# Gathered sums of a graph network: eight slots in the ring, addresses of a visit ahead of its waits

## The chip, the cores and the metric

The kernel runs on one core of a Trainium2 chip. The metric is the device time of one execution in microseconds (us), measured without the profiler; lower is better.

## The reference, cut to what matters

Four graph networks stand one behind the other on 3125 nodes with 256 features each, every one with a residual and a layer norm. The change touches the third, three relational layers over 18750 edges of 8 types:

```python
def _rgcn_layer(x, W, root, bias, src, dst, seg):
    agg = jax.ops.segment_sum(x[src], seg, num_segments=N_REL * N_NODES)
    agg = agg.reshape(N_REL, N_NODES, -1)
    return jnp.einsum('rnd,rde->ne', agg, W) + x @ root + bias
seg = edge_type * N_NODES + dst
h = x
for l in range(N_LAYERS - 1):
    h = jax.nn.relu(_rgcn_layer(h, weights[l], roots[l], biases[l], src, dst, seg))
h = jax.nn.sigmoid(_rgcn_layer(h, weights[-1], roots[-1], biases[-1], src, dst, seg))
```

## The kernel before, in words

**What a layer does.** For each node the products with all eight type matrices are written to a table in HBM; one row of the table is 3 x 256 bfloat16 values (a number split in three pieces). A layer then walks over the sorted edges in 25 tiles of 128 target nodes. For each chunk of 128 edges, GpSimd (POOL) gathers 128 table rows of 768 values with an indirect DMA (L2653), and TensorE (PE) multiplies them by a 0/1 matrix `hot` that DVE builds, so that the products add up in PSUM over the edges of a target node. Four chunks make a group, and a group of rows fills one slot of a ring `rows` of `R = SLOTS = 4` slots; `hot` and `lane` have a ring of the same length. `gather_sum` is called three times: `rel0s` and `rel1s` also compute the next layer's table while they sum (`then`), `rel2s`, the last, has only the sums.

**Counts.** 168 groups of four gathers in each layer, 672 gathers. A group whose edges end in one tile and begin in the next is used by both, so PE makes 191 visits of a group in a layer: 168 `add` and 23 `again`.

**Who waits for whom.** POOL waits, ahead of each group, for the group's indices (`s_at`, L2648, from DVE) and for the slot (`s_used`, L2649, from PE); L2650 stands behind both waits. With four slots group n may be gathered once PE has begun the visit of group n-3. SP waits for the 64 increments of each slot's semaphore and counts `s_landed` up by one (L2641). DVE computes row numbers (L2670, behind `s_landed`), target lanes (L2678) and `hot` (L2681), adds the finished tile (L2701, L2703), and prepares the next table (L2708, L2713, L2718), all in program order. PE visits a group: it waits for `s_hot` and `s_landed`, and issues for each of the four chunks a matmul of 512 columns (L2785) and one of 256 (L2788). Slots come from registers, so each operand needs its address worked out by PE's sequencer ahead of the matmul: in the order these are the rows `ISA` without a tile, in the trace the rows `FUSED_REGOPS`. In `rel0s` and `rel1s` PE puts between a visit's chunks the products for the next table (L2834) and, between tiles, sums counted edges (L3209, L3210) and closes each with a one-column matmul (L2814, L3211).

Of the kernel before, what the change touches and what calls it, by code (L numbers as in the profile page):

```python
# [6 lines left out]
P = 128  # L7
N = 3125
D = 256
# [22 lines left out]
SLOTS = 4  # L32
PIECES = 3
# [2559 lines left out]
def gather_sum(nc, name, g, table, own, out=None, then=None):  # L2593

    B, R = G_SUM, SLOTS
    WIDE = (REL + 1) * D
    NC = REL // 2
    with Phase(nc, name) as ph:
        rows = ph.sb("rows", [P, R, B, PIECES * D], BF16)
# [43 lines left out]
        @block.gpsimd  # L2643
        def _(pool):
            turns = turns_of(pool, g)
            with pool.Fori(0, turns, 1) as i:
                for u in range(R):
                    pool.wait_ge(s_at, i * R + (u + 1))  # L2648
                    pool.wait_ge(s_used, i * R + (u + 1))  # L2649
                    pool.sem_inc(g.waited, 1)  # L2650
                    for k in range(B):
                        n = u * B + k
                        pool.indirect_dma_start(rows[:, u, k, :], None, table,  # L2653
                                                bass.IndirectOffsetOnAxis(ap=at[:, n:n + 1], axis=0)).then_inc(s_in[u], 16)
# [108 lines left out]
        def _(pe):  # L2763
# [17 lines left out]
            def visit(a, hot_slot, row_slot, fresh, ends, after=None):  # L2781
                for k in range(B):
                    to = hot[:, bass.ds(hot_slot, 1), :, k].rearrange("p a n -> p (a n)")
                    row = rows[:, bass.ds(row_slot, 1), k, :].rearrange("p a d -> p (a d)")
                    one = nc.tensor.matmul(acc[a][:, :], to, row[:, 0:2 * D], start=fresh and k == 0, stop=False)  # L2785
                    if k == 0 and ends:
                        one.then_inc(s_used, 1)
                    last = nc.tensor.matmul(acc[a][:, D:2 * D], to, row[:, 2 * D:3 * D], start=False, stop=False)  # L2788
# [6 lines left out]
            def again(a):  # L2795
                v = pe.snap(seen, min_val=0, max_val=most)
                hot_slot = pe.snap(v % R)
                q = pe.snap(rows_in, min_val=0, max_val=most)
                row_slot = pe.snap((q + (R - 1)) % R)
                pe.wait_ge(s_hot, v + 1)  # L2800
                visit(a, hot_slot, row_slot, True, False)

            def add(a, fresh=False, after=None):
# [3 lines left out]
                row_slot = pe.snap(q % R)  # L2807
                pe.wait_ge(s_hot, v + 1)
                pe.wait_ge(s_landed, q + (R + 1))
                visit(a, hot_slot, row_slot, fresh, True, after)  # L2810
# [417 lines left out]
def program(nc, x, src, dst, kind, noise, gcn, local, ssm, mix, rel, last, out):  # L3228
    ctx = ExitStack()
    with ctx:  # L3230
# [45 lines left out]
        g.pool_sems = [ctx.enter_context(nc.semaphore(f"pool_dma{n}")) for n in range(36)]  # L3276
# [74 lines left out]
```

## Time and profile before

| | us |
|---|---|
| median of 3 timed runs | 7024.69 |
| lowest and highest of them | 7013.26, 7026.6 |
| span of the profiled execution | 7499.8 |

The profiled execution is one run with the recorder on; nothing of the program lies outside its span, so its own time is the 7499.8 us. It is 475.1 us longer than the median of the timed runs. Of the span PE is busy for 4435.1 us, DVE for 4012.2 us, POOL for 2382.3 us and ACT for 1792.5 us. The three relational sums take from 3515 to about 6640 us. A row's idle time is that of its engine just before it, and behind the arrow stands what ended it; "issue" is time in which the engine waited for nothing that the profile shows. PEld is the load of weights on TensorE, PEldq and POOLq are the instruction sequencers of these engines.

### The profile page before, as it was taken

How to read it: one execution, taken by the hardware profiler on the slowest of the kernel's cores; microseconds unless marked ns; L12 is line 12 of the kernel's file. 1: busy time of each engine (PE TensorE's matmuls, PEld its weight loads, DVE VectorE, ACT ScalarE, POOL GpSimd, SP SyncE). 2: the span in 40 equal slices, each digit the busy share in tenths (PEclk: the TensorE clock that was granted, in tenths of full speed). 3: DMA queues.
4: the chain of work that ended last, by engine and by line, in shares of the span. 5: the costliest groups of instructions: out<-in, count | busy, mean ns of one | idle time of the engine just before them, and what ended most of it. 6: DMA issues, size and time to landing. Idle time of an engine off the chain costs nothing. (4 is left out here: it accounts for less than half of the span.)

```text
span 7499.8 us, 87742 instructions
## 1 busy us (share of the span) xinstructions
PE 4435.1 (59%) x18992; PEld 2329.9 (31%) x19133; DVE 4012.2 (53%) x6257; ACT 1792.5 (24%) x2729; POOL 2382.3 (32%) x2285
## 2 busy tenths in 40 slices
PE   4888566217992554788456775556774444430583
PEld 2454465103441222654223332223331122220221
DVE  8986475898996695554222332223331111128895
ACT  1575112006882321443001111001110000010352
POOL 0000000400000353101666665666656666620000
PEclk8999687558995787899777887777886666665896
DMA  1471664326663575145555555555664444443443
GB/s 41 159 235 39 222 245 158 140 92 181 181 180 94 192 262 204 59 156 198 155 163 177 192 192 167 166 160 184 194 185 144 135 137 139 137 129 123 140 134 108
DMA packets 487888, 1181.10 MB, mean 157 GB/s; under 512 B 65242, under 2 KB 272293, under 8 KB 475138
## 3 DMA queue, kind: packets, MB, share of 16 engines
q1 hardware_dynamic: 313518, 570.19, 23.1%
q0 software_dynamic: 140880, 464.72, 20.5%
q10 hardware_dynamic: 33396, 145.09, 5.3%
q8 instruction: 41, 0.67, 0.0%
q14 instruction: 53, 0.43, 0.0%
HBM read 914.86 MB, written 268.11 MB: 158 GB/s over the span
## 5 line engine op out<-in xcount | busy, mean ns | idle before, releaser
L2653 POOL DMA_INDIRECT rel1s_rows<-rel_table,rel1s_at x672 | 652.1, 970 | 408.7 <-issue 345.7
L2653 POOL DMA_INDIRECT rel0s_rows<-rel_table,rel0s_at x672 | 653.7, 973 | 380.4 <-issue 346.6
L2653 POOL DMA_INDIRECT rel2s_rows<-rel_table,rel2s_at x672 | 648.1, 964 | 372.3 <-issue 333.1
L2785 PE MATMUL rel2s_acc<-rel2s_rows,rel2s_hot 128*128 x753 | 393.8, 537 | 469.6 <-issue 412.3
L2126 POOL TENSOR_TENSOR mamb_st<-mam_u,mamb_bc 128x1600 f32<-128x1600 f32 x64 | 230.8, 3606 | 1135.7 <-DMA mamb_bc<-dbc 1135.7
L1677 PE MATMUL gatx_acc<-gatx_w,gatx_feat 128*65 128x400 f32 x1600 | 541.6, 501 | 25.3 <-DVE gatx_w L1569 25.3
L2785 PE MATMUL rel0s_acc<-rel0s_rows,rel0s_hot 128*128 x740 | 332.8, 466 | 302.0 <-issue 212.6
L2785 PE MATMUL rel1s_acc<-rel1s_rows,rel1s_hot 128*128 x702 | 315.9, 464 | 275.9 <-issue 209.2
L1569 DVE SCALAR_TENSOR_TENSOR gatx_w<-gatx_w,gatx_adj 128x1600 f32<-128x1600 f32 x200 | 363.9, 1820 | 0.5 <-ACT gatx_w L1625 0.5
L1416 DVE CUSTOM_DVE_ANT_0 gatm_junk<-gatm_srow,gatm_gone 128x3200 bf16<-128x3200 f32 x100 | 343.5, 3489 | 33.5 <-DMA gatm_srow<-gat_scores 29.1
L1677 PE MATMUL latx_acc<-latx_w,latx_feat 128*65 128x400 f32 x800 | 291.3, 508 | 102.0 <-DVE latx_w L1569 102.0
L2171 PE MATMUL mamb_acc<-mamb_st,g_ident 128*128 128x512 f32 (+1 forms) x512 | 239.9, 623 | 150.5 <-DVE mamb_st L2159 150.5
L1677 PEld LDWEIGHTS gatx_acc<-gatx_w,gatx_feat 128*65 128x65 f32 x1600 | 221.2, 138 | 342.4 <-issue 315.6
L2678 DVE TENSOR_SCALAR rel2s_lane<-g_dsts,g_tile_base x168 | 43.0, 256 | 525.9 <-remote 392.3
L2788 PE MATMUL rel2s_acc<-rel2s_rows,rel2s_hot 128*128 x764 | 276.9, 362 | 67.0 <-issue 64.6
L438 PE MATMUL adj_acc<-adj_high,adj_low 128*128 x1196 | 269.3, 349 | 67.3 <-DVE adj_high L395 59.7
L2785 PEld LDWEIGHTS rel2s_acc<-rel2s_rows,rel2s_hot 128*128 x764 | 97.9, 128 | 660.2 <-issue 644.9
L395 DVE TENSOR_TENSOR adj_high<-adj_num,adj_mine 128x1600 f16 x299 | 296.2, 991 | 0.0
L2788 PE MATMUL rel1s_acc<-rel1s_rows,rel1s_hot 128*128 x764 | 245.1, 321 | 53.8 <-issue 44.0
L2678 DVE TENSOR_SCALAR rel1s_lane<-g_dsts,g_tile_base x168 | 40.6, 242 | 440.7 <-DMA dbc<-mamad_dbc 294.1
L2788 PE MATMUL rel0s_acc<-rel0s_rows,rel0s_hot 128*128 x764 | 244.7, 320 | 37.5 <-issue 35.2
L2678 DVE TENSOR_SCALAR rel0s_lane<-g_dsts,g_tile_base x168 | 42.5, 253 | 417.5 <-remote 224.3
(611 smaller groups left out, 9605.8 us busy)
## 6 DMA issues: line engine op xcount, KB each, us to landing
mamb_bc<-dbc SPq DMA_DIRECT2D x128, 800.0 KB, 5.8
agg_strip<-strips SPq DMA_DIRECT2D x100, 800.0 KB, 5.5
gatx_adj<-adj SPq DMA_DIRECT2D x200, 400.0 KB, 3.0
adj<-adj_counts SPq DMA_DIRECT2D x25, 1600.0 KB, 7.1
latx_adj<-adj SPq DMA_DIRECT2D x100, 400.0 KB, 3.0
rel_table<-rel0p_prod POOLq DMA_DIRECT2D x25, 1536.0 KB, 6.2
rel_table<-rel0s_prod ACTq DMA_DIRECT2D x25, 1536.0 KB
rel_table<-rel1s_prod ACTq DMA_DIRECT2D x25, 1536.0 KB
```

What stands on the lines that cost most here:

```text
L395: nc.vector.tensor_tensor(slot_of(high, slot).rearrange("p a k n q -> p (a k) n q"), num1[:, :, :].unsqueeze(1).to_broadcast([P, Q // 2, W ...
L438: last = nc.tensor.matmul(bank[:, 0:W16], low[:, bass.ds(slot, 1), :, i].rearrange("p a n -> p (a n)"), high[:, bass.ds(slot, 1), i // 2, ...
L1416: last = nc.vector.tensor_tensor_reduce(out=junk[:, h, :], in0=srow[:, h, :], in1=gone[u][:, :], scale=1.0, scalar=-3e38, op0=ALU.subtract ...
L1569: nc.vector.scalar_tensor_tensor(w[u][:, :, :], w[u][:, :, :], 1.0, adj[u][:, :].unsqueeze(1).to_broadcast([P, 2, J]), ALU.min, ALU.mult). ...
L1677: last = nc.tensor.matmul(acc[k][h][:, a, 0:J // 2], feat[u][:, h * 65:(h + 1) * 65], w[u][:, h, a * (J // 2):(a + 1) * (J // 2)], start=F ...
L2126: nc.gpsimd.tensor_tensor(st[q % RS][:, :], u[:, ct, when(half)], bc[r % RB][:, :], ALU.mult).then_inc(s_x, 1)
L2171: last = nc.tensor.matmul(acc[:, a:b], g.ident[:, :], st[q % RS][:, a:b], start=False, stop=n == S - 1)
L2653: pool.indirect_dma_start(rows[:, u, k, :], None, table, bass.IndirectOffsetOnAxis(ap=at[:, n:n + 1], axis=0)).then_inc(s_in[u], 16)
L2678: nc.vector.tensor_scalar(mine.rearrange("p a q -> p (a q)"), g.dsts[:, bass.ds(chunk, B)], base, None, ALU.subtract).then_inc(s_lane, 1)
L2785: one = nc.tensor.matmul(acc[a][:, :], to, row[:, 0:2 * D], start=fresh and k == 0, stop=False)
L2788: last = nc.tensor.matmul(acc[a][:, D:2 * D], to, row[:, 2 * D:3 * D], start=False, stop=False)
```

## The change

`SLOTS` goes from 4 to 8, so the rings of rows, indices, lanes and `hot` have eight slots, POOL's and SP's loops have eight groups in a turn (21 turns instead of 42), and 48 semaphores for DMAs are made instead of 36. The four chunks of a slot now lie in four tensors `rows0` to `rows3` instead of one. PE works out all addresses of a visit, four for the 512-column operands, four for the 256-column ones and four for `hot`, in one block ahead of the visit's two waits; the matmuls then follow each other with nothing between.

```diff
-SLOTS = 4
+SLOTS = 8
...
-        rows = ph.sb("rows", [P, R, B, PIECES * D], BF16)
+        rows = [ph.sb(f"rows{k}", [P, R, PIECES * D], BF16) for k in range(B)]
...
-                        pool.indirect_dma_start(rows[:, u, k, :], None, table,
+                        pool.indirect_dma_start(rows[k][:, u, :], None, table,
...
-            def visit(a, hot_slot, row_slot, fresh, ends, after=None):
+            def operands(hot_slot, row_slot):
+                of_row = lambda k: rows[k][:, bass.ds(row_slot, 1), :].rearrange("p a d -> p (a d)")
+                hots = [hot[:, bass.ds(hot_slot, 1), :, k].rearrange("p a n -> p (a n)") for k in range(B)]
+                most_two = [of_row(k)[:, 0:2 * D] for k in range(B)]
+                least = [of_row(k)[:, 2 * D:3 * D] for k in range(B)]
                 for k in range(B):
-                    to = hot[:, bass.ds(hot_slot, 1), :, k].rearrange("p a n -> p (a n)")
-                    row = rows[:, bass.ds(row_slot, 1), k, :].rearrange("p a d -> p (a d)")
-                    one = nc.tensor.matmul(acc[a][:, :], to, row[:, 0:2 * D], start=fresh and k == 0, stop=False)
+                    nc.tensor.lower_ap(most_two[k])
+                for k in range(B):
+                    nc.tensor.lower_ap(least[k])
+                for k in range(B):
+                    nc.tensor.lower_ap(hots[k], for_matmul_weights=True)
+                return hots, most_two, least
+
+            def visit(a, of_visit, fresh, ends, after=None):
+                hots, most_two, least = of_visit
+                for k in range(B):
+                    one = nc.tensor.matmul(acc[a][:, :], hots[k], most_two[k], start=fresh and k == 0, stop=False)
...
-                    last = nc.tensor.matmul(acc[a][:, D:2 * D], to, row[:, 2 * D:3 * D], start=False, stop=False)
+                    last = nc.tensor.matmul(acc[a][:, D:2 * D], hots[k], least[k], start=False, stop=False)
...
+                of_visit = operands(hot_slot, row_slot)
                 pe.wait_ge(s_hot, v + 1)
                 pe.wait_ge(s_landed, q + (R + 1))
-                visit(a, hot_slot, row_slot, fresh, True, after)
+                visit(a, of_visit, fresh, True, after)
...
-        g.pool_sems = [ctx.enter_context(nc.semaphore(f"pool_dma{n}")) for n in range(36)]
+        g.pool_sems = [ctx.enter_context(nc.semaphore(f"pool_dma{n}")) for n in range(48)]
```

On PE, one visit in the loop over a tile's groups in the last layer (`add`) reads before as follows; ISA is a register operation, REGISTER_ALU the one that makes the number waited for, so the first matmul stands behind the waits and two operations behind that row.

```order
L2804 ISA
L2809 REGISTER_ALU
L2785 ISA x2
L2785 MATMUL rel2s_acc1<-rel2s_rows,rel2s_hot 128x512
L2788 ISA
L2788 MATMUL rel2s_acc1<-rel2s_rows,rel2s_hot 128x256
L2785 ISA
L2785 MATMUL rel2s_acc1<-rel2s_rows,rel2s_hot 128x512
L2788 ISA
L2788 MATMUL rel2s_acc1<-rel2s_rows,rel2s_hot 128x256
```

The same visit in the changed kernel, where the lines are 12 to 14 higher from here on (the waits of L2808 to L2810 are now L2822 to L2824).

```order
L2817 ISA
L2787 ISA
L2789 ISA
L2791 ISA x2
L2823 REGISTER_ALU
L2797 MATMUL rel2s_acc1<-rel2s_rows0,rel2s_hot 128x512
L2800 MATMUL rel2s_acc1<-rel2s_rows0,rel2s_hot 128x256
L2797 MATMUL rel2s_acc1<-rel2s_rows1,rel2s_hot 128x512
L2800 MATMUL rel2s_acc1<-rel2s_rows1,rel2s_hot 128x256
L2797 MATMUL rel2s_acc1<-rel2s_rows2,rel2s_hot 128x512
```

The two operations behind the wait and the one ahead of every later matmul have moved to four rows ahead of the wait; the whole visit has 11 ISA rows' worth before and 6 now.

On POOL, the turn of the gathers of the last layer reads before as follows (one DMA row with x4 is a group).

```order
L3225 TENSOR_LOAD g_turns
L3225 ISA x2
L2646 UNCONDITIONAL_BRANCH
L2646 ISA
L2653 DMA rel2s_rows<-rel_table,rel2s_at 128x768 x4
L2648 REGISTER_ALU
L2653 DMA rel2s_rows<-rel_table,rel2s_at 128x768 x4
```

In the changed kernel the same place reads like this, and goes on for eight groups instead of four before the branch back.

```order
L3239 TENSOR_LOAD g_turns
L3239 ISA x2
L2646 UNCONDITIONAL_BRANCH
L2646 ISA
L2653 DMA rel2s_rows<-rel_table,rel2s_at 128x768 x4
L2648 REGISTER_ALU
L2653 DMA rel2s_rows<-rel_table,rel2s_at 128x768 x4
```

Nothing stands between a group's four gathers in either kernel; only the value that POOL waits for, and so how far it may run ahead of PE, is another.

## Rows read from the trace of the kernel before

**Rows 1.** Windows, all engines: the three relational sums, and the rest behind them.

```profile
core 0: us, PE busy (x) PEld busy (x) DVE busy (x) ACT busy (x) POOL busy (x), PEclk, DMA share, GB/s
3515.00:4575.00 1060.00, 675.14 (x2482) 325.09 (x2529) 305.31 (x826) 122.56 (x225) 653.71 (x672) 0.79 0.57 176
4575.00:5630.00 1055.00, 667.15 (x2448) 323.80 (x2511) 300.94 (x824) 122.85 (x225) 652.07 (x672) 0.78 0.56 175
5630.00:6640.00 1010.00, 460.82 (x1558) 198.88 (x1570) 181.98 (x603) 11.72 (x26) 648.07 (x672) 0.64 0.48 136
```

**Rows 2.** Gathers by tile: count, min/median/max ns, first and last start.

```profile
L2653 POOL DMA_INDIRECT rel0s_rows<-rel_table,rel0s_at x672: 943/949/1439, 3523.0 to 4542.9; - x168
L2653 POOL DMA_INDIRECT rel1s_rows<-rel_table,rel1s_at x672: 943/949/1443, 4580.6 to 5603.7; - x168
L2653 POOL DMA_INDIRECT rel2s_rows<-rel_table,rel2s_at x672: 943/949/1197, 5638.3 to 6624.0; - x168
```

**Rows 3.** Timeline of POOL, last layer: a steady stretch, then a gap.

```profile
6008.12 0.94 POOL L2653 DMA_INDIRECT rel2s_rows<-rel_table,rel2s_at  x1 [0.30 <-issue]
6009.36 0.95 POOL L2653 DMA_INDIRECT rel2s_rows<-rel_table,rel2s_at  x1 [0.30 <-issue]
6013.48 1.18 POOL L2653 DMA_INDIRECT rel2s_rows<-rel_table,rel2s_at  x1 [3.17 <-issue]
```

**Rows 4.** Timeline of PE at that gap, last layer.

```profile
6000.44 0.41 PE L2785 MATMUL rel2s_acc<-rel2s_rows,rel2s_hot 128*128 x1 [0.19 <-issue]
...
6001.65 0.27 PE L2788 MATMUL rel2s_acc<-rel2s_rows,rel2s_hot 128*128 x1
6003.20 0.40 PE L2785 MATMUL rel2s_acc<-rel2s_rows,rel2s_hot 128*128 x1 [1.28 <-issue]
...
6009.15 0.38 PE L2788 MATMUL rel2s_acc<-rel2s_rows,rel2s_hot 128*128 x1 [0.72 <-issue]
6013.00 0.61 PE L2785 MATMUL rel2s_acc<-rel2s_rows,rel2s_hot 128*128 x1 [3.48 <-issue]
```

**Rows 5.** Line L2788 on PE's sequencer in 6003 to 6009.5.

```profile
L2788 PEldq FUSED_REGOPS  x3: 691/709/726, 6004.8 to 6008.4; - x3
```

**Rows 6.** Line L2785 in 6003 to 6004.3: register operations and weights.

```profile
L2785 PEldq FUSED_REGOPS  x2: 8/11/14, 6004.1 to 6004.1; - x2
L2785 PEld LDWEIGHTS rel2s_acc<-rel2s_rows,rel2s_hot x1: 113/113/113, 6003.2 to 6003.2; 128*128 x1
```

**Rows 7.** Both lines' register operations over the whole last layer.

```profile
L2788 PEldq FUSED_REGOPS  x760: 2/46/1412, 5645.8 to 6627.1; - x190
L2785 PEldq FUSED_REGOPS  x950: 2/79/1395, 5645.5 to 6627.0; - x190
```

**Rows 8.** The same kind of operation in other loops, outside these layers.

```profile
L438 PEldq FUSED_REGOPS  x1196: 74/74/138, 80.2 to 556.0; - x200
L1675 PEldq FUSED_REGOPS  x60: 102/103/108, 1722.2 to 7341.7; - x60
```

**Rows 9.** DMA queues in 5640 to 6640: packets, MB, share.

```profile
q8 instruction: 2, 0.03, 0.0%
q14 instruction: 2, 0.02, 0.0%
```

**Rows 10.** Timeline of PE, first layer: a visit beside the next table, a bare one, the counted edges.

```profile
4346.12 1.02 PE L2834 MATMUL rel0s_mm<-rel0s_w,rel0s_turned 128*128 128x512 f32 x2
...
4347.30 1.02 PE L2834 MATMUL rel0s_mm<-rel0s_w,rel0s_turned 128*128 128x512 f32 x2
...
4354.09 0.38 PE L2785 MATMUL rel0s_acc<-rel0s_rows,rel0s_hot 128*128 x1
...
4355.39 0.17 PE L2814 MATMUL rel0s_acc<-g_zeros 128*128 128x1 bf16 x1
4355.64 0.27 PE L3210 MATMUL rel0s_dense<-rel0s_prod,rel0s_cnt 128*128 128x256 bf16 x1
...
4358.02 0.17 PE L3211 MATMUL rel0s_dense<-g_zeros 128*128 128x1 bf16 x1
```

**Rows 11.** Timeline of POOL and PE, end of the first layer and start of the second.

```profile
4542.94 0.94 POOL L2653 DMA_INDIRECT rel0s_rows<-rel_table,rel0s_at  x1 [0.30 <-issue]
...
4551.29 0.61 PE L2785 MATMUL rel0s_acc<-rel0s_rows,rel0s_hot 128*128 x1 [5.15 <-SPq L2641]
...
4580.65 0.94 POOL L2653 DMA_INDIRECT rel1s_rows<-rel_table,rel1s_at  x1 [36.76 <-DVE rel1s_at L2670]
```

More of the change, by code:

```diff
@@ L2799, in again @@
                 row_slot = pe.snap((q + (R - 1)) % R)
+                of_visit = operands(hot_slot, row_slot)
                 pe.wait_ge(s_hot, v + 1)
-                visit(a, hot_slot, row_slot, True, False)
+                visit(a, of_visit, True, False)
             def add(a, fresh=False, after=None):
@@ L2807, in add @@
                 row_slot = pe.snap(q % R)
+                of_visit = operands(hot_slot, row_slot)
                 pe.wait_ge(s_hot, v + 1)
                 pe.wait_ge(s_landed, q + (R + 1))
-                visit(a, hot_slot, row_slot, fresh, True, after)
+                visit(a, of_visit, fresh, True, after)
                 pe.reg_alu(rows_in, rows_in, 1, ALU.add)
```

## The prediction

> **What bounds the kernel now.** I read the windows first, for where the change acts: the three relational sums fill 1060, 1055 and 1010 us of the span, and in none of them is an engine full; POOL is busy for 653.71, 652.07 and 648.07 us, PE for 675.14, 667.15 and 460.82 us [rows 1]. So the question is who waits for whom. The gathers by tile give the frame: 672 in each layer, median 949 ns, from 3523.0 to 4542.9, 4580.6 to 5603.7 and 5638.3 to 6624.0 us [rows 2]. POOL's timeline gives their pace when nothing is in the way: 6008.12 to 6009.36, each 0.95 us and 0.30 us behind it, that is 1.25 us [rows 3]; in the same rows the next one comes 3.17 us late. 672 gathers at 1.254 us (0.30 us is rounded; four starts in a row give 5.01 us for a group) are 843 us, and POOL needs from the first start to the last end 1020.8, 1024.0 and 986.7 us. The difference is 178, 181 and 144 us. A part of it is longer gathers: 672 times 0.949 is 638 us, and the busy times lie 16, 14 and 10 us above that. What is left, 162 + 167 + 134 = 463 us, is POOL standing still ahead of a group.
>
> What it stands still for is in PE's timeline at the same place. A visit takes 6000.44 to 6001.65, about 1.5 us with its last matmul. The next one begins at 6003.20 and its last matmul at 6009.15, six us for the same eight matmuls, and the one after begins at 6013.00; 0.48 us later POOL goes on [rows 3, 4]. Within the slow visit the register operation of L2788 shows 691, 709 and 726 ns instead of its usual 46 [rows 5, 7]. With four slots POOL may not start group n before PE begins visit n-3, so a PE that falls back by 11.3 us (6001.65 to 6013.00) against a lead of at most 3 x 5.01 = 15 us, from which landing and what follows it go off (7.4 us from a last gather's end at 4543.88 to its visit at 4551.29 [rows 11]), stops POOL.
>
> **Are those gaps there without the recorder?** Here the argument turns. The profiled span is 7499.8 us and the median without profile is 7024.69, 475.1 less. Taking POOL's standstill out of the profiled span gives 7499.8 - 463 = 7037 us, with the longer gathers out too 6996 us; the timed 7025 lies between. Two further rows speak for the recorder. In the slow visit the register operations of L2785 have their records at 6004.1, while the weights that need the address were loaded at 6003.2 [rows 6]: the record came later than its use. And the same kind of operation takes 74 of at most 138 ns over 1196 cases, and 102 of at most 108 ns, in loops elsewhere [rows 8]; only where PE has eleven of them with eight matmuls and as many weight loads in a visit does it reach 1412 ns [rows 7]. I take it that the standstill belongs for the most part to the profiled execution, and that the timed kernel already gathers at close to POOL's own pace, 5.01 us a group.
>
> The Trainium skill ("NOTIFIC — the notification-queue block", section 7.1, Overflow) says that the block which writes the records always pushes back inside rather than lose one, and that this can throttle an engine. By that rule the gaps are the recorder's; the late records agree. The same page's section 10 (constraints, capacities, measured rates) says that a record costs the engine nothing; by that the gaps would be the program's, and the 1412 ns speak against it here.
>
> **The change part by part, against the timed 7025 us.**
>
> The ring of eight. POOL's lead over PE grows from three groups to seven, by 4 x 5.01 = 20 us. It saves only time in which POOL stands still for a slot. In the timed run that is what the recorder did not make. Its bounds are nothing and 463 us; the sum above leaves 7037 - 7025 = -12 us for it by the one count and 29 us by the other, so I take 4 us, and keep the ends. The work that covers a lead of three is PE's free time: in a layer with a next table a visit with its product takes 4347.30 - 4346.12 = 1.18 us for each of four chunks, a bare visit 1.30 us (4354.09 to 4355.39), counted edges 2.4 us a tile (4355.64 to 4358.02) [rows 10]. A tile has 191 / 25 = 7.6 visits; with eight products at 0.85 us (1.18 less a quarter of 1.30) and an estimate of 2.5 us for turns and roots, that is about 22 us at the full clock, against 168 / 25 x 5.01 = 34 us of gathers. PE is 12 us ahead in each tile. The windows show a granted clock of 0.79 and 0.78 [rows 1], by which 22 becomes 28 us, still less than 34; a tile wholly at the lower level of 1.2 GHz would be 44 us, 10 us late. In the last layer PE has only the visits, 10 us a tile, 20 at the lower level.
>
> Addresses in front of the waits. Two operations go from behind the wait: at 79 ns each 0.16 us [rows 7]. It matters only where PE waits for the rows and all wait for PE: at the end of a layer, where the last gather ends at 4543.88, its visit begins at 4551.29, and the next layer's first gather at 4580.65 [rows 11] (36.8 us later). 3 x 0.16 is 0.5 us; the 36.8 us chain itself stays. Elsewhere the operations between matmuls are hidden already: in a bare visit 4354.09 to 4355.39 eight matmuls follow each other with no idle time. Five fewer operations a visit cost or save the sequencer 5 x 0.06 = 0.3 us, hidden behind matmuls that are queued; the bound is 573 visits x 0.3 = 172 us of either sign.
>
> Four tensors instead of one, and the longer turns. POOL issues the same 672 gathers of the same size into other addresses, with nothing between a group's four. A branch comes once in eight groups instead of four, 21 times less in a layer for POOL and SP: under 63 x 0.1 = 6 us, and hidden for SP; I take 0.3 us. The next wait behind the gathers is DVE's: it makes row numbers in program order with the finished tile, so POOL cannot use all seven groups of lead anyway.
>
> Sum: 7025 - 4 - 0.5 - 0.3 = 7020 us.
>
> **The rivals.**
>
> *The gaps are real, and the ring takes them.* For it: the rows name POOL's waits, the standstill follows PE's slow visit, and the measured times need not share their cause with the profile's 475 us. Lead goes from 15 to 35 us against a delay of 11.3 us, so up to 463 us go, and at least 300 if DVE's order lets POOL lead by four or five groups only: 7025 - 463 = 6562 to 7025 - 300 = 6725, in the middle about 6640 us. Against it: the difference to the timed run would then have to come from elsewhere in the program by chance to within 12 us. What would make such gaps in a program is late instructions. In the last layer both instruction queues carry two packets each [rows 9], too few for gaps of this many microseconds in 168 groups.
>
> The Trainium skill ("Runtime: NRT & Kernel Launch", Instruction fetch mechanics) says that a taken branch to a page outside the loaded window stalls the engine for a fetch; by it PE's loops would make real gaps and the time would be that of this rival, 6640 us. The trace disagrees, with those two packets.
>
> *PE is late beside the next table.* The first two layers stand still for 28 and 33 us more than the last (162 and 167 against 134), and a tile at the lower clock is 10 us late by the count above. If this is so without the recorder, the ring saves these 61 us, or, with part of the last layer's, 75: 6950 to 6990, say 6975 us. Against it: PE records more operations in these layers, so the recorder could make this part as well.
>
> *The block in front is exposed.* All the addresses of a visit are now worked out before its first matmul may go. Where PE has nothing queued and the slot has already landed, the visit starts later by the 5 operations that were among the matmuls, 5 x 0.06 = 0.3 us, or 5 x 0.138 = 0.7 us by the longest of them in another loop [rows 8], and the 1.30 us visit becomes 1.6 to 2.0. That decides the time only if PE, not POOL, sets the pace of a stretch: from the point at which a tile of PE passes 34 us. With 28 us at the mean clock it needs 6 us more a tile, 0.8 us a visit. Where the clock is at the lower level it is passed. If a quarter of the 573 visits pay 0.3 to 0.7 us, that is 40 to 100 us; the ring gives some back. 7040 to 7110, say 7065 us.
>
> **How the numbers follow.** No change but the small sum, within 7005 to 7035: 0.58. PE late beside the table: 0.18. Gaps real: 0.12. Block exposed: 0.10. The rest, 0.02, is anything else. The range from 6950 to 7060 holds the first, nearly all of the second and half of the last, 0.58 + 0.17 + 0.05 = 0.80; it leaves out the case of 6640. 0.2% is 14 us, about what a measurement of this kernel can tell from no change. Faster by more: 0.18 x 0.95 + 0.12 + 0.05 of the first case's lower end = 0.34; slower 0.11; the same 0.55.
>
> **What the changed kernel's profile would show.** If I am right: gathers still 1.25 us apart between gaps, in the profiled run fewer or shorter gaps than 463 us in all, since eight slots also bridge the recorder's delays, so that the profiled span falls by far more than the timed median; the register operations of PE still slow in some stretches; the chain of 36.8 us between layers unchanged. The first rival: the timed median falls with the profiled span. The second: it falls by 35 to 75 us, with gaps gone in the first two layers in particular. The third: idle time of PE ahead of the first matmul of a visit grows, with slots landed. I am wrong at the root if the timed run also falls by hundreds of us, for then the standstill was not the recorder's.

## The result, and the profile after

The changed kernel takes 7039.21 us (median of 13 runs, 7036.99 to 7043.36) against 7026.6 us before (13 runs): ratio 1.0020, 95% interval 1.0013 to 1.0027. By the medians it is slower by 12.6 us, where the forecast was 7020 us, 5 us faster; the ratio is that of all runs and puts it at 0.20%. The time lies in the range of 6950 to 7060, on the side to which 0.11 had been given.

The kernel before has two levels, about 7027 us and about 7490 us. In each of the seven jobs of this document (a job is a set of kernels timed together) all its timed runs lie on one of them. The trace ahead of the prediction is of the long level, the timed runs beside it and the result are of the short one. Whether that trace was taken in the same job as those timed runs is not on record. A level isn't bound to the chip: one chip had the kernel before at 7028 us in one job and at 7483 in another.

The windows of the changed kernel, for the three relational sums (the columns are those of [rows 1]):

```profile
3515.00:4420.00 905.00, 628.50 (x2542) 319.24 (x2539) 310.95 (x828) 123.19 (x225) 651.76 (x672) 0.84 0.66 209
4420.00:5310.00 890.00, 625.48 (x2528) 320.06 (x2528) 308.87 (x826) 123.54 (x226) 650.61 (x672) 0.85 0.67 209
5310.00:6175.00 865.00, 438.93 (x1552) 188.11 (x1552) 182.68 (x599) 11.37 (x26) 644.94 (x672) 0.67 0.56 157
```

Its gathers by tile, which answer to [rows 2]:

```profile
L2653 POOL DMA_INDIRECT rel0s_rows<-rel_table,rel0s_at x672: 942/946/1457, 3527.3 to 4382.5; - x168
L2653 POOL DMA_INDIRECT rel1s_rows<-rel_table,rel1s_at x672: 942/946/1457, 4421.5 to 5275.5; - x168
L2653 POOL DMA_INDIRECT rel2s_rows<-rel_table,rel2s_at x672: 940/946/1187, 5311.6 to 6160.0; - x168
```

From first start to last end that is 856, 855 and 849 us, where [rows 2] gave 1021, 1024 and 987. There is no gap over 0.4 us between gathers in any of the three layers. The chain from a layer's last gather to the next one's first stays (POOL's timeline, for [rows 11]):

```profile
4382.55 0.95 POOL L2653 DMA_INDIRECT rel0s_rows<-rel_table,rel0s_at  x1 [0.31 <-issue]
4421.45 0.94 POOL L2653 DMA_INDIRECT rel1s_rows<-rel_table,rel1s_at  x1 [37.96 <-DVE rel1s_at L2670]
```

The address block of a visit costs 0.32 us in four operations of 74, 107 and twice 72 ns (TensorE's sequencer, last layer):

```profile
L2787 PEldq FUSED_REGOPS  x191: 74/74/79, 5310.9 to 6163.1; - x191
L2789 PEldq FUSED_REGOPS  x191: 105/107/107, 5311.1 to 6163.2; - x191
L2791 PEldq FUSED_REGOPS  x382: 60/72/79, 5311.2 to 6163.5; - x191
```

This looks as if the change had closed the gaps. It hadn't: the kernel before, profiled again at the short level (e9), has none either, and its gathers by tile fill 850, 851 and 841 us from the first start to the last:

```profile
L2653 POOL DMA_INDIRECT rel0s_rows<-rel_table,rel0s_at x672: 942/946/1413, 3528.4 to 4378.7; - x168
L2653 POOL DMA_INDIRECT rel1s_rows<-rel_table,rel1s_at x672: 942/946/1457, 4418.5 to 5269.8; - x168
L2653 POOL DMA_INDIRECT rel2s_rows<-rel_table,rel2s_at x672: 942/946/1092, 5305.9 to 6147.0; - x168
```

The comparison that counts is the busy time of the gathers in the two pages. The changed kernel:

```profile
L2653 POOL DMA_INDIRECT rel1s_rows<-rel_table,rel1s_at x672 | 650.6, 968 | 242.4 <-issue 191.9
L2653 POOL DMA_INDIRECT rel2s_rows<-rel_table,rel2s_at x672 | 644.9, 960 | 239.5 <-issue 195.0
L2653 POOL DMA_INDIRECT rel0s_rows<-rel_table,rel0s_at x672 | 651.8, 970 | 217.6 <-issue 190.4
```

The kernel before, at the same level (e9):

```profile
L2653 POOL DMA_INDIRECT rel1s_rows<-rel_table,rel1s_at x672 | 647.9, 964 | 243.3 <-issue 196.5
L2653 POOL DMA_INDIRECT rel0s_rows<-rel_table,rel0s_at x672 | 646.7, 962 | 217.8 <-issue 195.9
L2653 POOL DMA_INDIRECT rel2s_rows<-rel_table,rel2s_at x672 | 637.6, 949 | 239.6 <-issue 202.3
```

The sum is 1947.3 against 1932.2 us: the same 2016 gathers take 15.1 us longer. The time rose by 12.6. In both traces POOL never stands still for longer than its usual 0.3 us within these layers, so each longer gather counts in full. One trace against another of nearly the same kernel can differ by some 2 us in this sum (e3, below, has 1934.5).

### The profile page after: what moved, and what is told of

The parts are those of the page before. It is cut to its first block and busy times, and to the rows that moved or that the text cites. A ratio compares the mean times of both kernels' runs of the same rounds, so it can differ in the third digit from the quotient of the medians.

```text
span 7040.2 us, 84702 instructions
## 1 busy us (share of the span) xinstructions
PE 4328.9 (61%) x19132; PEld 2310.2 (33%) x19133; DVE 4026.1 (57%) x6257; ACT 1793.2 (25%) x2729; POOL 2375.5 (34%) x2285
## 5 line engine op out<-in xcount | busy, mean ns | idle before, releaser
L2797 PE MATMUL rel2s_acc<-rel2s_rows,rel2s_hot 128*128 x764 | 404.9, 544 | 425.9 <-SPq L2641 423.9
L2797 PE MATMUL rel0s_acc<-rel0s_rows,rel0s_hot 128*128 x764 | 314.9, 435 | 261.7 <-SPq L2641 260.2
L2797 PE MATMUL rel1s_acc<-rel1s_rows,rel1s_hot 128*128 x764 | 313.1, 433 | 261.7 <-SPq L2641 261.3
L2797 PEld LDWEIGHTS rel2s_acc<-rel2s_rows,rel2s_hot 128*128 x764 | 100.3, 131 | 646.6 <-SPq L2641 518.9
L2800 PE MATMUL rel2s_acc<-rel2s_rows,rel2s_hot 128*128 x764 | 281.7, 369 | 0.0
L2701 DVE TENSOR_TENSOR rel2s_res<-rel2s_acc,rel_own 128x256 f32<-128x256 f32 x24 | 10.2, 424 | 443.8 <-PE rel2s_acc L2828 443.8
L890 PE MATMUL agg_acc<-agg_split,agg_strip 128*128 128x192 bf16 (+1 forms) x2500 | 235.9, 252 | 0.1
L2800 PE MATMUL rel0s_acc<-rel0s_rows,rel0s_hot 128*128 x764 | 232.2, 304 | 0.0
L2800 PE MATMUL rel1s_acc<-rel1s_rows,rel1s_hot 128*128 x764 | 231.9, 304 | 0.0
L2797 PEld LDWEIGHTS rel0s_acc<-rel0s_rows,rel0s_hot 128*128 x764 | 90.8, 119 | 422.0 <-SPq L2641 308.6
```

What stands on the lines that cost most here:

```text
L890: last = nc.tensor.matmul(acc[u][:, 0:W], strip[u][:, s * P:(s + 1) * P], split[:, s, :], start=False, stop=False)
L2701: nc.vector.tensor_tensor(res[u][:, :], acc[u][:, 0:D], own_of(t), ALU.add).then_inc(s_part, 1)
L2797: one = nc.tensor.matmul(acc[a][:, :], hots[k], most_two[k], start=fresh and k == 0, stop=False)
L2800: last = nc.tensor.matmul(acc[a][:, D:2 * D], hots[k], least[k], start=False, stop=False)
```

## The experiments

All are edits of the kernel before or of the changed one; times are medians, ratios are to the kernel before in the same job. "Gathers" is the busy time of the 2016 gathers in the kernel's one trace, "still" what the gaps over 0.4 us between them are longer than the usual 0.3 us. The ratio goes by all runs, so it need not be that of the two medians (e1: 1.0017 by medians).

| run | level | us | ratio (95%) | gathers | still |
|---|---|---|---|---|---|
| the change | short | 7039.2 | 1.0020 (1.0013 to 1.0027) | 1947.3 | 0 |
| e1 ring of eight alone | short | 7040.3 | 1.0021 (1.0012 to 1.0030) | 1945.8 | 1 |
| e2 addresses alone | short | 7023.9 | 0.9991 (0.9982 to 1.0000) | 1931.3 | 0 |
| e3 48 semaphores alone | short | 7027.8 | 0.9998 (0.9989 to 1.0007) | 1934.5 | 0 |
| e4 less matmul work | short | 7040.9 | 1.0016 (1.0007 to 1.0025) | 1945.0 | 0 |
| e5 rows 8, hot 4 | short | 7033.5 | 1.0009 (1.0000 to 1.0018) | 1938.2 | 0 |
| e6 rows 4, hot 8 | short | 7023.3 | 0.9994 (0.9985 to 1.0003) | 1928.2 | 0 |
| e7 change, hot in four operations | short | 7107.7 | 1.0116 (1.0101 to 1.0132) | 2016.7 | 0 |
| e8 e2, hot in four operations | short | 7095.5 | 1.0097 (1.0082 to 1.0113) | 2002.6 | 0 |
| e9 kernel before, one run | short | 7028.1 | | 1932.2 | 0 |
| e10 e2 with hot 8 | short | 7024.7 | 0.9996 (0.9987 to 1.0005) | 1931.6 | 1 |
| e11 change, short hot | short | 7016.8 | 0.9984 (0.9975 to 0.9993) | 1918.0 | 0 |
| e12 e2, short hot | short | 7011.6 | 0.9977 (0.9967 to 0.9986) | 1914.8 | 0 |
| e13 e2, hot in halves | long | 7460.1 | 0.9935 (0.9921 to 0.9948) | 1925.1 | 450 |
| e14 change, hot from PSUM, layer 3 | long | 7706.9 | 1.0269 (1.0255 to 1.0283) | 1935.3 | 687 |
| e15 the change again | long | 7623.2 | 1.0186 (1.0166 to 1.0206) | 1945.1 | 582 |
| e16 addresses alone again | long | 7431.3 | 0.9929 (0.9915 to 0.9943) | 1949.1 | 396 |
| e17 ring of eight alone again | long | 7739.9 | 1.0350 (1.0335 to 1.0365) | 1948.0 | 694 |
| e18 ring of three, addresses | long | 7471.9 | 0.9986 (0.9977 to 0.9995) | 1945.5 | 435 |

Subtract gathers and standstill from the time: 5091 to 5099 us is left in all thirteen rows of the short level, and 5085 to 5098 in the six of the long one. Whatever was changed on TensorE, DVE or in the rings moved the time through one of these two columns.

**The parts of the change, one by one.** e1 is the ring alone, with the 48 semaphores that come with it (e2 goes back to 36):

```diff
-SLOTS = 4
+SLOTS = 8
```

> The ring of eight slots with the addresses of before (one tensor of rows, register operations between the matmuls) and 48 semaphores. Theory A (the standstill of 463 us was the recorder's, caused by eleven register operations among the matmuls of each visit; the timed run gathers at POOL's pace): the timed median stays within 15 us of 7026; the profiled execution may still be slow on TensorE's sequencer, but eight slots bridge part of it, so its span falls below 7400 us. Theory B (the 13 us that the change costs come from the deeper ring: more gathers in flight, longer landings): timed 7036 to 7042. Theory C (they come from the address block ahead of the waits): timed 7020 to 7030.

e2 is the changed kernel with the ring put back:

```diff
-SLOTS = 8
+SLOTS = 4
```

> Ring of four as before, but the rows in four tensors and all addresses of a visit ahead of its waits. Theory A: with six register operations a visit and none among the matmuls the recorder keeps up, so that the profiled span falls from 7499.8 us to within 20 us of the timed median. If instead the deeper ring had closed the gaps, the span stays above 7300 us. Theory B (the ring costs the 13 us): timed 7020 to 7030. Theory C (the block costs them): timed 7036 to 7042.

e3 only makes 48 semaphores for 36:

> The kernel before with 48 semaphores for DMAs made instead of 36 and nothing else changed. If the 13 us have to do with the relational layers at all (theories B and C), this is within 5 us of before. Theory D (they come from outside these layers, from the numbers of semaphores and what the barriers clear): timed 7036 or more.

Measured by the medians: e1 +11.9 us, e2 -4.4, e3 -0.5. The ring costs what the change costs, as theory B has it (its reason, more gathers in flight, is taken up below), the addresses with the four tensors at best give a little back, and C and D fall. Theory A stood in one point and fell in another: e1, e2 and e3 all have profiled spans within 3 us of their medians (7038.3, 7026.4, 7026.5), though e1 and e3 have the old register operations among the matmuls. So these operations alone do not make a profile long. Nor does recording by itself, at either level: in each of e1 to e18 the profiled span lies within 10 us of the kernel's timed median.

**Is TensorE late?** e4 cuts the second matmul of a chunk from 256 to 16 columns:

```diff
-last = nc.tensor.matmul(acc[a][:, D:2 * D], to, row[:, 2 * D:3 * D], start=False, stop=False)
+last = nc.tensor.matmul(acc[a][:, D:D + 16], to, row[:, 2 * D:2 * D + 16], start=False, stop=False)
```

> The kernel before with the 256-column matmul of each chunk cut to 16 columns (it leaves most of the third piece's product out), so that TensorE has 4 x 0.1 us less to do in each of 573 visits, 229 us in all. Theory A (POOL's gathers set the pace of the timed run): timed within 6 us of before, since only the visits at the layers' ends count. Theory E (TensorE is late in the timed run too, at least beside the next table): 20 to 75 us less.

Less work on TensorE made it slower, 12.6 us by the medians and 11 by the ratio, so E falls; A's "within 6 us" falls too. The table says where it went: the gathers take 1945.0 us, 10 more than in e3, nearly all in the last layer (646.6 against 637.9).

**What makes a gather longer.** DVE and POOL in the last layer of the changed kernel (timeline), the first two of four `hot` in a row:

```profile
5820.44 0.43 DVE L2681 TENSOR_TENSOR rel2s_hot<-g_lanes,rel2s_lane 128x512 f16 x1
5820.60 1.09 POOL L2653 DMA_INDIRECT rel2s_rows<-rel_table,rel2s_at  x1 [0.30 <-issue]
5820.89 0.17 DVE L2670 COPY rel2s_at<-g_rows  x1
5821.34 0.34 DVE L2678 TENSOR_SCALAR rel2s_lane<-g_dsts,g_tile_base  x1 [0.28 <-issue]
5821.82 0.43 DVE L2681 TENSOR_TENSOR rel2s_hot<-g_lanes,rel2s_lane 128x512 f16 x1 [0.15 <-DVE rel2s_lane L2678]
5821.99 1.08 POOL L2653 DMA_INDIRECT rel2s_rows<-rel_table,rel2s_at  x1 [0.30 <-issue]
```

And in the kernel before at the short level (e9), where hot comes once in a group:

```profile
5707.07 0.23 DVE L2678 TENSOR_SCALAR rel2s_lane<-g_dsts,g_tile_base  x1 [2.93 <-PE rel2s_acc L2788]
5707.44 0.42 DVE L2681 TENSOR_TENSOR rel2s_hot<-g_lanes,rel2s_lane 128x512 f16 x1
5708.09 0.95 POOL L2653 DMA_INDIRECT rel2s_rows<-rel_table,rel2s_at  x1 [0.30 <-issue]
```

A gather that starts while `hot` is being made mostly takes 1.08 us, nearly all others 0.946. I counted, for each gather, what DVE was doing at its start (layers one to three; "long" is over 1.0 us; "extra" is for `hot` alone; counts move by a few with how the edges of an operation are taken, the long ones hardly):

```
kernel        hot at the start (long)   extra us   other two-source operation, L2718 (long)
e3, as before   60, 62, 20 (53, 53, 20)    19.7    46, 46 (20, 19)
e1, ring 8      70, 80, 71 (65, 76, 71)    31.3    46, 46 (18, 20)
e4, less PE     63, 74, 82 (59, 72, 79)    32.1    46, 46 (18, 21)
change          79, 75, 73 (75, 74, 66)    32.7    45, 46 (15, 17)
```

31.3 less 19.7 is 11.6 us: the whole 11.9 of the ring. DVE's operations with one source in PSUM (L2701, L2703, L2708, L2713) lie over 64 to 84 starts in each of the first two layers of e3, e1 and the change, and at most three of all those gathers are long.

The traces show more than the meeting: POOL waits for `hot` to end. In the change, e1, e3, e4 and e9 there are 877 long gathers under `hot`, and each ends 0.81 to 0.83 us behind the end of its `hot`, which began 0.045 to 0.174 us ahead of the gather. A `hot` that begins later than that leaves the gather at 0.946 us and may itself be held up: those that begin in the last 0.044 us ahead of a start all end 0.45 to 0.46 us behind it. So what counts is which of the two is first, and how long `hot` then has to go.

The chain of waits of DVE, 5330 to 6130 us, shows why the ring changes that count. Changed kernel:

```profile
DVE rel2s_res L2701 <- PE rel2s_acc L2828: 397.5, 22, 20.5
DVE rel2s_at L2670 <- SPq L2641: 71.9, 31, 3.8
```

Kernel before (e9):

```profile
DVE rel2s_at L2670 <- SPq L2641: 355.1, 159, 4.5
DVE rel2s_lane L2678 <- PE rel2s_acc L2788: 218.0, 99, 2.9
```

With four slots DVE waits in nearly each of the 160 groups of this stretch for the landing, and in 99 for the visit, and so makes `hot` at much the same place in a group of gathers, mostly a harmless one. With eight it does a tile's groups ahead, waits up to 20.5 us for TensorE to end the tile, and then works its backlog off in a burst, every 1.39 us, in step with gathers of 1.08 + 0.30 us: each of the four `hot` of this burst meets a gather's start.

The step is no chance either, since POOL holds DVE in turn. In the rows above `lane` takes 0.34 instead of 0.23 us and ends at 5821.68, with the gather (5821.69); `hot` follows 0.14 us later, and so 0.17 us ahead of the next gather, which comes 0.30 us behind the last. Of the change's 215 long gathers under `hot` 176 follow a `lane` that ended within 0.025 us of the gather before. Once DVE has nothing else to wait for, each of the two sets the other's next meeting.

**Is it the depth, or the phase?** e5 and e6 part the rings:

```diff
-B, R = G_SUM, SLOTS
+B, R, H = G_SUM, 8, 4       # e6: 4, 8
-lane = ph.sb("lane", [P, R, B], F16)
-hot = ph.sb("hot", [P, R, P, B], BF16)
+lane = ph.sb("lane", [P, H, B], F16)
+hot = ph.sb("hot", [P, H, P, B], BF16)
```

> Rows and indices in a ring of eight, lanes and hot in a ring of four, addresses as before. Theory F (the 12 us of the deeper ring are gathers made longer by DVE: with eight slots of hot DVE runs ahead to a tile's end, waits there for up to 20 us and then makes several hot tiles in a burst, of which one that begins in the gap between two gathers makes the next gather 0.14 us longer; with four slots PE's visits keep DVE in one phase of the group): DVE is held by PE's visit four back again, so the sum of the last layer's gathers falls from 645 to about 638 us and the timed median to 7026 to 7031. Theory G (the depth of the row ring itself, more gathers in flight): the gathers stay at 645 us and the time at 7036 to 7042.

> Rows and indices in a ring of four, lanes and hot in a ring of eight, addresses as before. Theory F: DVE's row numbers wait for a landing four groups back, so DVE is still held to the gathers' pace; 7026 to 7034, with the last layer's gathers at 638 to 642 us. If it is the depth of hot alone that lets DVE burst, they are at 645 us and the time at 7036 to 7042.

In e5 the last layer's gathers are back at 638.3 us with eight row slots: phase, not depth (F), for that layer. Its time, 7033.5, is halfway and outside both forecasts: the first two layers stay at 649.6 and 650.3, with 64 and 72 gathers that start under `hot`; why the hold does not reach them is open. e6 holds DVE by the landings alone and has the least gather time of the kernels that leave `hot` as one whole operation, 1928.2 us (636.9 in the last layer); its time, 7023.3, is below its forecast. DVE's longest waits in the stretch from 5330 to 6130 us show what holds it, e5 first:

```profile
DVE rel2s_lane L2678 <- PE rel2s_acc L2788: 574.6, 161, 5.8
```

```profile
DVE rel2s_at L2670 <- SPq L2641: 500.3, 159, 4.2
```

e4 points the same way: its ring has four slots, only TensorE is changed, and 82 gathers of its last layer start under `hot`.

e11 and e12 cut `hot` to 16 of 128 columns, in the changed kernel and in e2, which leaves out most of the sums:

```diff
-nc.vector.tensor_tensor(hot[:, bass.ds(slot, 1), :, :]..., g.lanes[:, :, :],
-                        mine.to_broadcast([P, P, B]), ALU.is_equal).then_inc(s_hot, 1)
+nc.vector.tensor_tensor(hot[:, bass.ds(slot, 1), 0:16, :]..., g.lanes[:, 0:16, :],
+                        mine.to_broadcast([P, 16, B]), ALU.is_equal).then_inc(s_hot, 1)
```

> The changed kernel with hot's operation cut to 16 of its 128 columns (hot is cleared at a layer's start and the rest of it stays zero, so most of the sums are left out). Theory F: no hot operation lies over a gather's start for long, the gathers of the last layer fall from 645 to about 636 us and those of the first two by about 11 us each; with 3 x 2 to 4 us for clearing hot the time is 7010 to 7022, the same as the next kernel's but for the clearing. Theory G (depth by itself costs): it stays 10 us above the next kernel's.

> Ring of four with four row tensors and the addresses in front, with the same short hot. Theory F: gathers of the last layer 636 us, of the first two 638 to 641; 7004 to 7016 with the clearing of half as much.

No gather is longer under `hot` any more: it now takes 0.19 us and is over before it can hold a gather back. The 15.3 us between the ring of eight and that of four (the change against e2, by medians of two jobs; 17.0 by their differences to the kernel before) shrink to 5.2, of which 3.2 are gathers; the clearing of a ring twice as large is in the rest. The short `hot` is still made from two sources in SBUF, so the sources alone do not make a gather long.

**Which property of the operation?** e7 and e8 make `hot` in four operations with one tensor and one scalar per partition, from float32 lanes:

```diff
-lane = ph.sb("lane", [P, R, B], F16)
+lane = ph.sb("lane", [P, R, B], F32)
...
+for k in range(B):
+    one = nc.vector.tensor_scalar(hot[:, bass.ds(slot, 1), :, k]..., g.lanes[:, :, k],
+                                  lane[:, bass.ds(slot, 1), k], None, ALU.is_equal)
```

> The changed kernel (ring of eight, addresses in front), but hot made by four operations with one tensor as source and the lane as a scalar for each partition, instead of one operation with two tensors from SBUF. Theory F with the shared way of DVE and POOL into SBUF as the cause: the gathers no longer stretch under hot, the last layer's sum falls from 645 to about 636 us, and the time from 7039 to 7015 to 7028. Theory G: no change in the gathers, 7036 to 7045, or more by DVE's longer work.

> Ring of four with four row tensors and the addresses in front, and hot made by four operations with one tensor as source. Theory F: the collisions under hot in the first two layers go too (some 5 of the 26 us by which gathers are longer there, the rest being under other operations of DVE), 7010 to 7022. If DVE's longer work, four operations for one, makes POOL or PE wait: slower than 7028.

The opposite of what F expected: 68 and 72 us slower than the kernels they were made from, by 69 and 71 us of gathers. The channel is the right one, my idea of what is harmless in it was not. The extra begins at `lane` (L2678), which writes float32 now: in e7's last layer 78 gathers start under it, all are long, by 0.46 us each. But `lane` alone is not what POOL waits for. The 10 gathers of that layer that start between `lane` and the first of the four `hot` operations, under no operation of DVE, are all long too, and the layer's 105 long gathers end on average 0.88 us (standard deviation 0.01) behind the start of the second `hot`, whenever they started. POOL is held over `lane` and the first `hot` together; which of the two does it, and by what property, no run parts. One of these gathers (timeline of e7):

```profile
5708.85 0.23 DVE L2678 TENSOR_SCALAR rel2s_lane<-g_dsts,g_tile_base  x1 [0.28 <-issue]
5708.87 1.45 POOL L2653 DMA_INDIRECT rel2s_rows<-rel_table,rel2s_at  x1 [0.30 <-issue]
5709.24 0.96 DVE L2682 TENSOR_SCALAR rel2s_hot<-g_lanes,rel2s_lane 128x128 f16 x4 [0.15 <-DVE rel2s_lane L2678]
```

e14 leaves the operation as it is in the changed kernel and moves one source of it to PSUM, in the last layer:

```diff
+of_psum = ph.ps("lanes", [P, BANK])[:, :].rearrange("p (n q) -> p n q", q=B)
...
-g.lanes[:, :, :],
+g.lanes[:, :, :] if then else of_psum,
```

> The changed kernel, where in the last layer alone (the only one with a PSUM bank free) hot's first source is a copy of the lane numbers in PSUM as float32, the second still in SBUF. Theory F with two sources from SBUF as what POOL cannot work beside: none of the 73 gathers whose start hot lies over is long any more although hot itself takes about 0.7 instead of 0.43 us; the last layer's gathers fall from 645 to 636 us, the first two layers stay at 651, time 7028 to 7032. If any DVE operation of this length lies in the way: the last layer's gathers at 645 us or more, 7039 to 7050.

It ran at the long level, so its time says nothing on this, but its gathers do. `hot` is longer there:

```profile
L2686 DVE TENSOR_TENSOR rel2s_hot<-rel2s_lanes,rel2s_lane x191: 691/692/693, 5833.7 to 6817.8; 128x512 f32 x191
```

Yet of 106 gathers that start under it none is long, where e15, the change itself at the same level, has 69 of 77. The rows of the last layer in their pages, e14 first:

```profile
L2655 POOL DMA_INDIRECT rel2s_rows<-rel_table,rel2s_at x672 | 635.2, 945 | 390.4 <-issue 209.8
```

```profile
L2653 POOL DMA_INDIRECT rel2s_rows<-rel_table,rel2s_at x672 | 646.0, 961 | 369.6 <-issue 205.3
```

So whether `hot` holds POOL hangs on both its sources being in SBUF, and how long it does on when `hot` ends. (The source in PSUM is float32 as well; but L2718, with a float32 and a 16-bit source both in SBUF, also makes gathers long, so the type is not what sets POOL free.) The Trainium skill ("SBUF — State Buffer", section "SBUF: two separate sides") has the mechanism: DVE and GpSimd share a pair of ports into SBUF under an exclusive lock, held for the whole operation by whichever starts first, and a DVE operation with two SBUF inputs contends for it with a GpSimd operation that reads SBUF. The gather reads its row numbers, `at`, there. By that rule one source in PSUM sets POOL free, and the 106 gathers agree; that the first to start holds the other up agrees with the 877 above. That it is this pair of ports, and not another thing that the two engines share, no run shows.

**A version better than both.** e10 joins e2 and e6, e13 makes `hot` in two halves on e2:

> Addresses in front and four row tensors as in the change, rows in a ring of four, lanes and hot in a ring of eight. Theory F: DVE is held to the gathers by its row numbers and fewer hot tiles fall on a gather's start; the two small gains (0.09% of the addresses, 0.06% of this ring pair) add up at best: 7018 to 7024. If both were noise: 7024 to 7030.

> Addresses in front and ring of four, hot made by two operations of 64 of its 128 columns each (0.25 us instead of one of 0.43). Theory F: a hot operation that begins in the gap lies over the next gather's start for a shorter time, so that the 17 us by which hot lengthens the gathers fall to 8 to 12: gathers 1931 to about 1925 us in all, time 7016 to 7022. If only whether an operation lies over the start counts and not for how long, the number of starts met stays or grows with two operations: 7022 to 7032.

e10 (7024.7) is no better than e2 (7023.9) or e6 (7023.3) and just outside the 7018 to 7024 of added gains: the two small gains do not add, and each is at the edge of what can be told. e13's gathers are down to 1925.1 us as forecast (e16, without halves, has 1949.1 at that level), but it ran at the long level; its ratio of 0.9935 is no better than that of e16 (0.9929), so a gain in time is not shown.

**The long level.** e9 was made to see whether the 475 us of the first profile come back:

> The kernel before, unchanged, profiled once more. If the 475 us by which its profiled execution was longer than the timed ones belong to that one execution, the span is 7020 to 7035 us and POOL never stands still between gathers. If they belong to this kernel whenever it is recorded, the span is above 7300 us again.

They did not: the span is 7026.3 us, with no gap. Then the job of e13 and e14 had the kernel before at 7507 us in nine timed runs of nine, and the next two jobs at 7483 and 7482.

> The changed kernel, unchanged. On a chip where the kernel before takes 7027 us: 7036 to 7042 again. On a chip where it takes 7507: theory H (slow stretches of the sequencers there are few and longer with eight slots, since DVE and PE work in bursts and then both stand): 7600 to 7750. Theory A (slots bridge them): below 7200.

> Ring of four, addresses in front, as in e2. On a chip of 7027 us: 7018 to 7027. On a chip of 7507: 7440 to 7490, as fewer register operations of TensorE fall into slow stretches (e13 had 318 slow ones on TensorE where the profile of before had 727).

> Ring of eight with the addresses of before, as in e1. On a chip of 7027 us: 7036 to 7044. On a chip of 7507: theory H 7600 or more, theory A below 7250.

At this level the ring of eight costs 257 us, the addresses in front save 52, and the change costs 140; e15 and e17 lie where theory H had them, e16 is 9 us below its forecast. A longer ring doesn't bridge the gaps, it comes with fewer and longer ones: 29 to 34 a layer of 4.5 to 8.4 us (e14, e15, e17) instead of 30 to 49 of 3 to 4 (e16). The gathers' sums hardly differ (1945.1, 1949.1 and 1948.0 us), so at this level the differences are standstill. With eight slots, and in e13, DVE's sequencer is slow as well; its register operations in front of `lane`, e15 and then e16:

```profile
L2678 DVEq FUSED_REGOPS  x861: 2/153/1396, 3523.4 to 6716.8; - x173
```

```profile
L2678 DVEq FUSED_REGOPS  x861: 14/149/218, 3530.7 to 6540.4; - x173
```

In all these traces a stretch of register operations over 0.5 us has ended by 3 to 7 us after POOL stopped, which suggested that the gathering keeps it up. e18, a ring of three, was to test that:

> Ring of three slots, addresses in front. Theory H (at the long level a stretch of slow register operations lasts as long as POOL goes on gathering and ends within 3 us of its stop, so that a longer ring makes longer stretches): if the kernel before takes about 7490 us in this job, the stretches are shorter still than with four slots, 7300 to 7425; if slots bridged them, above 7500. If the kernel before takes about 7027: POOL then stands still where TensorE is late beside the next table, 7025 to 7060, with the gathers' sum at 1925 to 1935.

Theory H falls: 7471.9 us is neither of the two forecasts for this level. The slow operations of TensorE are down to 55 (222 in e16), but POOL stands still for 435 us, more than with four slots (396). So the number of slow operations does not set how long POOL stands. One of its 186 gaps (timeline of e18):

```profile
6052.60 0.41 PE L2797 MATMUL rel2s_acc<-rel2s_rows,rel2s_hot 128*128 x1 [1.34 <-issue]
...
6054.43 0.17 DVE L2670 COPY rel2s_at<-g_rows  x1
6054.53 0.95 POOL L2653 DMA_INDIRECT rel2s_rows<-rel_table,rel2s_at  x1 [0.30 <-issue]
6057.63 0.62 PE L2797 MATMUL rel2s_acc<-rel2s_rows,rel2s_hot 128*128 x1 [3.54 <-SPq L2641]
...
6059.24 1.02 POOL L2653 DMA_INDIRECT rel2s_rows<-rel_table,rel2s_at  x1 [3.76 <-issue]
```

With three slots the group of 6059.24 needs the visit of 6052.60, which by the record was there 2.9 us before POOL was ready (6055.48). POOL goes on 1.6 us after the next visit. By the records the signal was given, and POOL did not go on with it. What sets a job's level, and what delays such signals, stays open.

## Why the prediction was wrong, step by step

**The standstill.** The forecast took the 463 us out of the timed run, and rightly for that run: at the short level POOL never stands still, and 7037 by subtraction is near the 7027 of the timed runs. But the reason was wrong, and that the forecast came out near is luck in this point. "I take it that the standstill belongs for the most part to the profiled execution": the kernel before took 7483 to 7507 us in all timed runs of three of the six jobs of experiments, and every kernel profiled in an experiment has a span within 10 us of its timed median, at either level. It is a level of the job. That is also why the profiled span fell by far more than the timed median, from 7499.8 to 7040.2 us, as I had said it would: the two traces are of different levels. Late records [rows 6] were no proof of a recorder that holds the engines up, and the Trainium skill's rule on how records push back, which I let speak for it, is shown by no run here. My sign of being wrong at the root, that the timed run falls by hundreds of us, could not have found this out, since both timed runs were of the short level. (The 3.17 us in [rows 3] hold the usual 0.30, so that gather comes 2.87 us late; the sum does not rest on it.)

**The ring, -4 us.** This is the step that failed: the sum had the ring save 4 us, and it costs 11.9 (e1), 11.6 of them counted as longer gathers. "It saves only time in which POOL stands still for a slot" left out that the ring also moves DVE. I asked only what waits the lead would remove. The 41 us of longer gathers were in my own first paragraph, 16, 14 and 10 by layer [rows 1, 2], and I took them out of the sum without asking what makes a gather longer; the answer was DVE, for which POOL waits inside a gather, and whatever moves DVE in time moves that number.

**"Cannot use all seven groups of lead anyway".** Beside the point: POOL stood still for no slot at the short level and needed none of them. DVE used them, to run ahead to the tile's end.

**The addresses, -0.5 us.** -4.4 us, interval 0 to -13 (e2): right in sign, the size can't be told from mine. The cause can't either: e2's gathers are 0.9 us shorter than e9's and 3.2 shorter than e3's, which may be part of it.

**Semaphores and branches, -0.3 us.** -0.5 us for the semaphores (e3, interval -8 to +5), as small as taken. The 0.1 us for a branch in the bound of 6 us is shown by no run, and the branches were not tried by themselves.

**The rivals.** The gaps bridged by the ring, 6640 us: false at the short level, where there are none, and reversed at the long one, where the gaps are real and the kernel with the longer ring takes 257 us more. TensorE late beside the table, 6975: false, at the short level POOL never stood still in the first two layers, and less work on TensorE (e4) gained nothing. The exposed block, 7065: the right side by the wrong mechanism; the block costs 0.32 us a visit and e2 is not slower. No rival named the meeting of DVE and POOL.

## What to carry to other kernels

Where an engine never waits, ask what makes each of its operations longer, not only what it waits for: a mean of 973 ns beside a median of 949 (the first layer of the kernel before) is a term of the sum. A deeper ring is not only lead for its consumer; every engine that was held in step by the short ring is set free, and may then work in bursts that meet another's operations. Compare the span of a profile with the timed runs first, and where they differ by more than 1%, profile again before reading waits from it.

## What was not expected of the hardware

A gather that starts 0.045 to 0.174 us behind the start of a `hot` with two SBUF sources waits for it, and takes 1.08 instead of 0.946 us; with one source in PSUM it takes 0.946 (0 of 106 longer). Where `lane` is float32 and `hot` is four one-tensor operations, a gather that starts under `lane` takes 1.41 (e7). `lane` in turn is held until a gather ends, and this brings the next `hot` ahead of the next gather. A program on one core had two levels, 7027 and 7490 us, constant within a job and not tied to the chip; at the long one only the stretch of the three relational sums is longer (its first gather starts at 3523 and 3528 us, and 875 and 878 us are left behind its last, in the first trace and in e9).
